# Scatters and gathers alternated by column in the first edge stage of a four-layer graph network, and VectorE's broadcast columns read as per-partition scalars

## The chip, the cores and the metric

The kernel runs on one core of a Trainium2 chip. The metric is the device time of one execution in microseconds (us), the median of several runs. Before the change three runs gave 5754.19, 5760.32 and 5761.99 us.

## The reference, cut to what matters

Four graph layers run one after the other on 3125 nodes of 128 features and 100,000 edges sorted by destination. Each layer gathers a row per edge from a table of the nodes, computes on it, and sums or maximises the rows by destination. Two parts matter here.

```python
# layer 0: both directions of every edge, so one sum is by dst and one by src
mi  = concat([node[src_bi], node[tgt_bi], ef_bi], 1)
h   = relu(layernorm(mi @ w1 + b1)) @ w2 + b2
agg = segment_sum(h, tgt_bi)
# layer 1: a softmax over the edges of one source, summed by destination
seg_max = segment_max(e, src);  p = exp(e - seg_max[src]);  p = p / segment_sum(p, src)[src]
agg = segment_sum(norm_h[src] * p[:, None], dst)
```

The source statistics that layer 1 needs (maximum, sum of exponentials) are collected while layer 0 walks over the edges.

## The kernel before, in words

The edges are padded to 784 columns of 128. A batch is four columns (CB = 4, 512 edges), so a stage over the edges has 196 batches (NBAT); two batches are a group (C2 = 8 columns). Each of the five engines has an order of work written out by hand: one loop over i, in which batch i - k is handled by step k of the pipeline, with semaphores between engines. Nothing is planned at run time.

**First edge stage (`L0_edges`).** GpSimd (POOL) issues indirect DMAs. `pool_gather` (line 1180) fetches, for each of the 128 edges of a column, a row of 256 floats of the table T0 into the ring `Gs` of eight buffers; the first gather of a batch waits until TensorE has read the buffer's previous batch (`T`). `pool_scatter` (line 1161) adds a column of 132 floats per edge into one of three tables `tabs`, chosen by column number modulo three; each scatter waits until the one three columns earlier has landed (`tab`), and the first of a batch waits for its data (`X`, written by ScalarE, lines 1075 and 1076). In round i POOL issues the four scatters of batch i - 9, then `pool_outside` (for this data one no-op that sets `ok`, line 1174), then the four gathers of batch i. Rounds 0 to 8 have no scatters, rounds 196 to 204 no gathers. Rounds 1 to 6 also issue a few small gathers (`pool_sub`, line 1187).

ScalarE's round begins with `act_X`, which waits for all four scatters of the batch three earlier, because the buffer `X2` has three parts. VectorE (DVE) adds the gathered rows to TensorE's products (`dve_t`, line 875), builds a mask of equal sources within a column (`dve_S1`, line 892), scales five of the eight half columns by their rstd (`dve_D`, line 951; ScalarE does the other three), and in every second round builds the one-hot matrices for the source statistics (`dve_A`, lines 956 to 964). In `dve_S1`, `dve_D` and `dve_A` a column of one number per edge is spread over a whole tile by the helper `bf`, as the second input of a `tensor_tensor`; `bc` repeats a row. Line 974 (`dve_OT`) already uses a `tensor_scalar` with a per-partition scalar.

**Second edge stage (`L1_edges`).** Of every seven batches POOL gathers six with line 1525 (`edge_gather`, ring of eight buffers), the seventh comes from TensorE by one-hot matrices. `dve_scale` (line 1733) multiplies the gathered 512 numbers per partition by a broadcast column `pp`; it is followed, in every second round, by lines 1737 and 1741. The third and fourth edge stages use line 1525 too.

Of the kernel before, what the change touches and what calls it, by code (L numbers as in the profile page):

```python
# [6 lines left out]
P = 128  # L7
N = 3125
NBLK = 25
# [5 lines left out]
CB = 4  # L15
C2 = 2 * CB
C4 = 4 * CB
NBAT = NCH // CB
# [3 lines left out]
KT = 3  # L22
# [13 lines left out]
ALU = mybir.AluOpType  # L36
# [115 lines left out]
def bc(v, n=NBLK):  # L152
    return v.unsqueeze(1).to_broadcast([P, n, v.shape[1]])


def bf(v, f=P):
    return v.unsqueeze(2).to_broadcast([P, v.shape[1], f])
# [6 lines left out]
def at_rows(ap):  # L164
    return bass.IndirectOffsetOnAxis(ap=ap, axis=0)
# [17 lines left out]
def build(nc, A, out):  # L183
    with ExitStack() as ctx:
# [10 lines left out]
        arena = Arena(sb("arena", [AW]), AW)  # L195
# [7 lines left out]
        iotaf = sb("iotaf", [P])  # L203
# [478 lines left out]
        def L0_edges():  # L682
# [28 lines left out]
            mg = [arena.get(C2) for _ in range(4)]  # L711
            sg = [arena.get(C2) for _ in range(4)]
            OL = arena.get(C2, P)
            OH = arena.get(C2, NBLK)
            fst = arena.get(C2)
            RH = arena.get(C2, 2, NBLK)
            DM = [arena.get(C2 + 1, NBLK) for _ in range(2)]
            DS = [arena.get(C2 + 1, NBLK) for _ in range(2)]
# [167 lines left out]
            def dve_S1(e, b):  # L886
                g, h0 = b // 2, b % 2 * CB * P
                if b % 2 == 0:
                    e.wait_ge(ld_s.of(g), ld_s.at(g))
                if b >= 6:  # L890
                    e.wait_ge(SS.of(0), SS.at(b - 6))
                e.tensor_tensor(Sm[b % 6], sR[g % 3][:, h0:h0 + CB * P].rearrange("p (c f) -> p c f", f=P),
                                bf(srcF[:, CB * b:CB * b + CB]), ALU.is_equal).then_inc(S1.of(0), 1)

            def dve_dm(e, b):
                g = b // 2
# [50 lines left out]
            def dve_D(e, b):  # L947
                g, o = b // 2, b % 2 * C2
                e.wait_ge(rs.of(0), rs.at(g * (RS + 1) + RS))
                t = Gs[b % NR].rearrange("p c (h f) -> p (c h) f", h=2)[:, 0:C2 - ND, :]  # L950
                e.tensor_tensor(t, t, bf(rst[g % 3][:, o:o + C2 - ND]), ALU.mult).then_inc(D.of(0), 1)

            def dve_A(e, b):
                g = b // 2
                sl = slice(C2 * g, C2 * g + C2)
                e.tensor_tensor(OL, bc(iotaf[:, :], C2), bf(loF[:, sl]), ALU.is_equal)
                e.tensor_tensor(OH, bc(iotaf[:, 0:NBLK], C2), bf(hiF[:, sl], NBLK), ALU.is_equal)
                e.tensor_scalar(fst, cb[g % 4], 0.5, None, ALU.is_lt).then_inc(A1.of(0), 1)
                e.wait_ge(A1.of(0), A1.at(2 * g))
                e.tensor_tensor(OH, OH, bf(fst, NBLK), ALU.mult).then_inc(A1.of(0), 1)  # L960
                e.wait_ge(A1.of(0), A1.at(2 * g + 1))
                e.wait_ge(ex.of(0), ex.at(b))
                e.tensor_tensor(RH[:, :, 0, :], OH, bf(mg[g % 4], NBLK), ALU.mult)
                e.tensor_tensor(RH[:, :, 1, :], OH, bf(sg[g % 4], NBLK), ALU.mult).then_inc(RHd.of(0), 1)

            def dve_S4(e, b):
                e.wait_ge(S3.of(0), S3.at(b))
# [184 lines left out]
                    if 0 <= i - 7 < NBAT and (i - 7) % 2:  # L1152
                        act_DX(e, i - 7)

            def pool_scatter(e, b):
                e.wait_ge(X.of(0), X.at(b))
                for c in range(CB):
                    k = CB * b + c
                    if k >= KT:
                        e.wait_ge(tab.of(k), tab.at(k - KT))  # L1160
                    e.indirect_dma_start(out=tabs[k % KT], out_offset=at_rows(iA[b % 10][:, c:c + 1]),  # L1161
                                         in_=X2[b % 3][:, c, :], in_offset=None, compute_op=ALU.add
                                         ).then_inc(tab.of(k), 16)

            def pool_outside(e, b, some):
                with e.If(some > 0):
# [6 lines left out]
                    e.wait_ge(gx.of(0), gx.at(b))  # L1173
                e.engine_nop().then_inc(ok.of(0), 1)  # L1174

            def pool_gather(e, b):
                if b >= NR:
                    e.wait_ge(T.of(0), T.at(b - NR))
                for c in range(CB):
                    e.indirect_dma_start(out=Gs[b % NR][:, c, :], out_offset=None, in_=T0,  # L1180
                                         in_offset=at_rows(srcI[:, CB * b + c:CB * b + c + 1])
                                         ).then_inc(gs.of(b), 16)

            def pool_sub(e, b0, b1):
                dFc = dF.rearrange("(s i) -> s i", i=P)
# [5 lines left out]
            def pool(e):  # L1191
                meet(e)
                some = e.value_load(flag[0:1, 0:1], min_val=0, max_val=EP)
                for i in range(NBAT + 9):
                    if i == 9:
                        e.wait_ge(st_zero.of(0), st_zero.at(KT - 1))
                    if 0 <= i - 9 < NBAT:
                        pool_scatter(e, i - 9)
                    if 0 <= i - 1 < NBAT:
                        pool_outside(e, i - 1, some)  # L1200
                    if i < NBAT:
                        pool_gather(e, i)
                    if 1 <= i <= 6:
                        pool_sub(e, 4 * (i - 1), 4 * i + (i == 6))
                for k in range(NCH - KT, NCH):
                    e.wait_ge(tab.of(k), tab.at(k))
# [408 lines left out]
        def L1_edges():  # L1615
# [114 lines left out]
            def dve_scale(e, b):  # L1730
                g_ = rows_of(b)
                e.wait_ge(ex.of(0), ex.at(b))
                e.tensor_tensor(g_[:, :, 0:P], g_[:, :, 0:P], bf(pp[b % 4]), ALU.mult).then_inc(D.of(0), 1)

            def dve_cut_r(e, g):
                e.wait_ge(c1.of(0), c1.at(g))
# [768 lines left out]
```

## Time and profile before

| | us |
|---|---|
| median of three runs | 5760.32 |
| the profiled execution's own time | 5759.2 |
| its span, first to last instruction | 5757.4 |
| POOL busy | 4263.1 (74%) |
| TensorE matmuls busy | 4205.9 (73%) |
| VectorE busy | 4170.5 (72%) |
| ScalarE busy | 3607.3 (63%) |

The span holds the preparation of the edge lists, four edge stages and four short node stages. In the profile the first edge stage runs from about 50 to 2692 us (scatters from 151.5 us, gathers until 2622 us), the second from 2799 to about 3687 us, the third from 3754 to about 4780 us and the fourth from 4860 to about 5700 us. A POOL interval in the trace is the time in which GpSimd writes the descriptors of one indirect DMA; the data lands later, and is not part of it. "issue" is idle time that nothing in the profile explains.

### The profile page before, as it was taken

How to read it: one execution, taken by the hardware profiler on the slowest of the kernel's cores; microseconds unless marked ns; L12 is line 12 of the kernel's file. 1: busy time of each engine (PE TensorE's matmuls, PEld its weight loads, DVE VectorE, ACT ScalarE, POOL GpSimd, SP SyncE). 2: the span in 40 equal slices, each digit the busy share in tenths (PEclk: the TensorE clock that was granted, in tenths of full speed). 3: DMA queues.
4: the chain of work that ended last, by engine and by line, in shares of the span. 5: the costliest groups of instructions: out<-in, count | busy, mean ns of one | idle time of the engine just before them, and what ended most of it. 6: DMA issues, size and time to landing. Idle time of an engine off the chain costs nothing.

```text
span 5757.4 us, 83215 instructions
## 1 busy us (share of the span) xinstructions
PE 4205.9 (73%) x23301; PEld 3141.9 (55%) x23378; DVE 4170.5 (72%) x10652; ACT 3607.3 (63%) x12260; POOL 4263.1 (74%) x3819
## 2 busy tenths in 40 slices
PE   3766666676666666665688888658888886999995
PEld 2656666565656565654455555435555554545453
DVE  4877677777777777774788888757777776777776
ACT  3766676767666666763477777447676763555553
POOL 4788888888888888887477777567777763777776
PEclk6877778777777777777799998879999997999997
DMA  8876767676666667675367767456666762555553
GB/s 253 168 170 161 173 159 174 160 169 163 166 167 165 167 162 170 163 171 99 100 192 195 194 197 195 140 169 213 210 211 209 213 198 72 157 156 161 160 158 107
DMA packets 629376, 976.86 MB, mean 170 GB/s; under 512 B 105688, under 2 KB 339026, under 8 KB 628642
## 3 DMA queue, kind: packets, MB, share of 16 engines
q1 hardware_dynamic: 394242, 616.02, 33.9%
q0 software_dynamic: 234656, 355.35, 29.8%
q8 instruction: 192, 3.15, 0.2%
q14 instruction: 286, 2.34, 0.1%
HBM read 668.28 MB, written 306.11 MB: 169 GB/s over the span
## 4 chain that ended last, share of the span: by engine, by line
POOL 60%; issue 21%; PE 6%; DMA 4%; DVE 4%; SPq 1%; POOLq 1%; ACT 1%; DVEq 0%; ACTq 0%
POOL arena L1525 32%; POOL tab L1161 16%; POOL arena L1180 12%; DMA tab<-arena 2%; DMA arena<-T,srcI 1%; POOLq L1174 1%; PE PS L2012 1%; PE PS L1688 1%; POOL arena L1213 1%; PE PS L301 1%; PE PS L1483 0%; SPq L786 0%; PE PS L1990 0%; PE PS L813 0%; PE PS L833 0%
## 5 line engine op out<-in xcount | busy, mean ns | idle before, releaser
L1525 POOL DMA_INDIRECT arena<-T,srcI x2112 | 2034.7, 963 | 787.7 <-issue 636.3
L1161 POOL DMA_INDIRECT tab<-arena x784 | 1290.3, 1646 | 276.9 <-issue 231.1
L1180 POOL DMA_INDIRECT arena<-T,srcI x784 | 804.5, 1026 | 285.6 <-issue 282.2
L1512 DVE TENSOR_TENSOR_SCAN arena<-arena,PS 128x512 f32<-128x512 bf16 x588 | 748.9, 1274 | 183.4 <-PE PS L2326 81.5
L852 PE MATMUL PS<-arena 128*128 128x128 f32 x1568 | 308.7, 358 | 679.7 <-ACT arena L1108 679.7
L1492 ACT ACTIVATE arena<-PS 128x512 f32<-128x512 f32 x588 | 347.4, 591 | 642.8 <-PE PS L1483 642.8
L1592 DVE TENSOR_SCALAR arena<-PS,nodeid 128x512 bf16<-128x512 f32 x908 | 627.9, 739 | 75.4 <-PE PS L1573 75.4
L852 PEld LDWEIGHTS PS<-arena 128*128 128x128 f32 x1568 | 265.8, 256 | 719.0 <-ACT arena L1108 719.0
L933 DVE CUSTOM_DVE_ANT_0 arena<-arena,ltri 128x128 f32<-128x128 f32 x784 | 225.1, 287 | 495.4 <-ACT arena L1084 495.3
L833 PE MATMUL PS<-We,arena 65*128 65x256 f32 x1568 | 511.3, 409 | 87.5 <-DVE arena L875 43.6
L1688 PE MATMUL PS<-arena 128*128 128x396 bf16 x2800 | 544.9, 353 | 7.4 <-DVE arena L1592 7.2
L2308 PE MATMUL PS<-arena 128*128 128x512 bf16 x2323 | 545.2, 382 | 4.3 <-issue 0.2
L1075 ACT ACTIVATE arena<-arena 128x4 f32<-128x4 f32 x196 | 40.7, 208 | 756.5 <-DMA tab<-arena 753.1
L835 PE MATMUL PS<-arena 128*128 128x256 f32 x1568 | 490.8, 395 | 0.0
L1126 ACT ACTIVATE arena<-arena 128x128 bf16<-128x128 f32 x1568 | 459.6, 300 | 40.6 <-DVE arena L875 40.6
L1483 PEld LDWEIGHTS PS<-ident,arena 128*128 128x128 f32 x2352 | 289.4, 145 | 323.2 <-issue 264.8
L1483 PE MATMUL PS<-ident,arena 128*128 128x128 f32 x2352 | 371.8, 282 | 120.2 <-ACT arena L1492 118.7
L1688 PEld LDWEIGHTS PS<-arena 128*128 128x128 bf16 x2800 | 289.3, 104 | 218.4 <-issue 50.0
L1612 ACT ACTIVATE arena<-arena,onesF 128x512 bf16<-128x512 f32 x592 | 402.1, 712 | 6.0
L1607 ACT ACTIVATE arena<-arena,minus 128x512 f32<-128x512 f32 x592 | 400.0, 709 | 0.0
L2032 DVE TENSOR_TENSOR arena<-arena,PS 128x1024 f32<-128x1024 f32 x196 | 238.7, 1218 | 218.8 <-DMA arena<-T,srcI 217.8
L2012 PE MATMUL PS<-arena,wA 128*128 128x512 f32 x784 | 392.9, 625 | 0.0
(302 smaller groups left out, 10279.1 us busy)
## 6 DMA issues: line engine op xcount, KB each, us to landing
H<-arena SPq DMA_DIRECT2D x784, 256.0 KB, 2.5
arena<-keepR SPq DMA_DIRECT2D x294, 256.0 KB, 5.0
arena<-sF SPq DMA_DIRECT2D x98, 512.0 KB, 5.6
arena<-wF SPq DMA_DIRECT2D x98, 512.0 KB, 7.1
arena<-dF SPq DMA_DIRECT2D x98, 512.0 KB, 8.5
arena<-T,srcI POOLq DMA_INDIRECT x2896, 3.5
arena<-in_ea64T SPq DMA_DIRECT2D x98, 256.0 KB
arena<-S SPq DMA_DIRECT2D x98, 256.0 KB
```

The lines of the kernel that those rows point to most:

```text
L833: e.matmul(psC[:, c * 2 * P:(c + 1) * 2 * P], eT[g % 3][0:65, h0 + c * P:h0 + (c + 1) * P], We[0:65, :], start=True, stop=False)
L835: ins = e.matmul(psC[:, c * 2 * P:(c + 1) * 2 * P], OT[b % 2][:, c * P:(c + 1) * P], Tw[g % 4], start=False, stop=True)
L852: ins = e.matmul(bank(6)[:, c * P:(c + 1) * P], Sm[b % 6][:, c, :], R2[b % 2][:, c, :], start=True, stop=True)
L1126: ins = e.activation(ja[:, 2 * c + hh, :], t[:, c, hh * P:(hh + 1) * P], ACT.Square, accum_out=var[g % 3][:, i:i + 1])
L1161: e.indirect_dma_start(out=tabs[k % KT], out_offset=at_rows(iA[b % 10][:, c:c + 1]), in_=X2[b % 3][:, c, :], in_offset=None, compute_op=AL ...
L1180: e.indirect_dma_start(out=Gs[b % NR][:, c, :], out_offset=None, in_=T0, in_offset=at_rows(srcI[:, CB * b + c:CB * b + c + 1])).then_inc(g ...
L1483: ins = e.transpose(psB[b % n][:, (c * nh + h) * P:(c * nh + h + 1) * P], s[b % len(s)][:, h, c * P:(c + 1) * P], ident[:, :])
L1512: ins = e.tensor_tensor_scan(s[b % n][:, h, :], kR[g % 6][:, h0:h0 + CB * P], src[h], s[(b - 1) % n][:, h, CB * P - 1:CB * P] if b else in ...
L1525: e.indirect_dma_start(out=dst[:, c, :], out_offset=None, in_=T_tab, in_offset=at_rows(srcI[:, CB * b + c:CB * b + c + 1])).then_inc(gs.of ...
L1592: e.tensor_scalar(self.OH[j % 2][:, n, :], self.sB[j % len(self.sB)], nodeid[:, n:n + 1], None, ALU.is_equal).then_inc(self.oh.of(0), 1)
L1688: ins = e.matmul(psP[:, c, 0:3 * XW], pk.OH[j % 2][:, n, c * P:(c + 1) * P], part[:, n, :, :].rearrange("p k f -> p (k f)"), start=(n == 0 ...
L2308: ins = e.matmul(bank(4 + j % 2), part[k][:, n, :], pk.OH[j % 2][:, n, :], start=(n == 0 and k == 0), stop=(n == NBLK - 1 and k == 2))
```

## The change

In `L0_edges`, scatters and gathers are issued in turn, column by column, after `pool_outside`, which was between them before. The three VectorE steps replace one wide `tensor_tensor` by one `tensor_scalar` per column (four in `dve_S1`, five in `dve_D`, eight for `OL` in `dve_A`), whose scalar is the column itself. In `dve_A` the matrix `OH` is gone: two small products `first` (eight columns by two) are made instead, and eight `scalar_tensor_tensor` of 50 elements write `RH` directly. In `L1_edges`, `dve_scale` is split in four `tensor_scalar` in the same way.

```diff
@@ dve_S1
-                e.tensor_tensor(Sm[b % 6], sR[g % 3][:, h0:h0 + CB * P].rearrange("p (c f) -> p c f", f=P),
-                                bf(srcF[:, CB * b:CB * b + CB]), ALU.is_equal).then_inc(S1.of(0), 1)
+                for c in range(CB):
+                    k = CB * b + c
+                    ins = e.tensor_scalar(Sm[b % 6][:, c, :], sR[g % 3][:, h0 + c * P:h0 + (c + 1) * P], srcF[:, k:k + 1],
+                                          None, ALU.is_equal)
+                ins.then_inc(S1.of(0), 1)
@@ dve_D
-                t = Gs[b % NR].rearrange("p c (h f) -> p (c h) f", h=2)[:, 0:C2 - ND, :]
-                e.tensor_tensor(t, t, bf(rst[g % 3][:, o:o + C2 - ND]), ALU.mult).then_inc(D.of(0), 1)
+                t = Gs[b % NR].rearrange("p c (h f) -> p (c h) f", h=2)
+                for k in range(C2 - ND):
+                    ins = e.tensor_scalar(t[:, k, :], t[:, k, :], rst[g % 3][:, o + k:o + k + 1], None, ALU.mult)
+                ins.then_inc(D.of(0), 1)
@@ dve_A
-                sl = slice(C2 * g, C2 * g + C2)
-                e.tensor_tensor(OL, bc(iotaf[:, :], C2), bf(loF[:, sl]), ALU.is_equal)
-                e.tensor_tensor(OH, bc(iotaf[:, 0:NBLK], C2), bf(hiF[:, sl], NBLK), ALU.is_equal)
                 e.tensor_scalar(fst, cb[g % 4], 0.5, None, ALU.is_lt).then_inc(A1.of(0), 1)
+                for c in range(C2):
+                    k = C2 * g + c
+                    e.tensor_scalar(OL[:, c, :], iotaf[:, :], loF[:, k:k + 1], None, ALU.is_equal)
                 e.wait_ge(A1.of(0), A1.at(2 * g))
-                e.tensor_tensor(OH, OH, bf(fst, NBLK), ALU.mult).then_inc(A1.of(0), 1)
+                e.wait_ge(ex.of(0), ex.at(b))
+                e.tensor_tensor(first[:, :, 0], fst, mg[g % 4], ALU.mult)
+                e.tensor_tensor(first[:, :, 1], fst, sg[g % 4], ALU.mult).then_inc(A1.of(0), 1)
                 e.wait_ge(A1.of(0), A1.at(2 * g + 1))
-                e.wait_ge(ex.of(0), ex.at(b))
-                e.tensor_tensor(RH[:, :, 0, :], OH, bf(mg[g % 4], NBLK), ALU.mult)
-                e.tensor_tensor(RH[:, :, 1, :], OH, bf(sg[g % 4], NBLK), ALU.mult).then_inc(RHd.of(0), 1)
+                for c in range(C2):
+                    k = C2 * g + c
+                    ins = e.scalar_tensor_tensor(out=RH[:, c, :, :], in0=bc(iotaf[:, 0:NBLK], 2), scalar=hiF[:, k:k + 1],
+                                                 in1=bf(first[:, c, :], NBLK), op0=ALU.is_equal, op1=ALU.mult)
+                ins.then_inc(RHd.of(0), 1)
@@ pool, L0_edges (pool_scatter and pool_gather now take one column c; their waits on X and T stand at c == 0)
-                    if 0 <= i - 9 < NBAT:
-                        pool_scatter(e, i - 9)
                     if 0 <= i - 1 < NBAT:
                         pool_outside(e, i - 1, some)
-                    if i < NBAT:
-                        pool_gather(e, i)
+                    for c in range(CB):
+                        if 0 <= i - 9 < NBAT:
+                            pool_scatter(e, i - 9, c)
+                        if i < NBAT:
+                            pool_gather(e, i, c)
@@ dve_scale, L1_edges
-                e.tensor_tensor(g_[:, :, 0:P], g_[:, :, 0:P], bf(pp[b % 4]), ALU.mult).then_inc(D.of(0), 1)
+                for c in range(CB):
+                    ins = e.tensor_scalar(g_[:, c, 0:P], g_[:, c, 0:P], pp[b % 4][:, c:c + 1], None, ALU.mult)
+                ins.then_inc(D.of(0), 1)
```

## Rows read from the trace of the kernel before

**Rows 1.** Windows of both stages: length, busy us of PE, PEld, DVE, ACT, POOL
```profile
151.00:2622.00 2471.00, 1658.18 (x9080) 1494.76 (x9079) 1793.47 (x7004) 1700.41 (x7665) 2001.17 (x1496) 0.78 0.69 165
2799.00:3673.00 874.00, 743.67 (x4381) 473.94 (x4381) 713.85 (x1189) 629.49 (x1278) 669.20 (x672) 0.91 0.68 190
```
**Rows 2.** The chain that ended last, whole span, by engine
```profile
POOL 60%; issue 21%; PE 6%; DMA 4%; DVE 4%; SPq 1%; POOLq 1%; ACT 1%; DVEq 0%; ACTq 0%
```
**Rows 3.** Who waited for whom, 300 to 2600 us: total, times, longest
```profile
ACT arena L1075 <- DMA tab<-arena: 691.7, 88, 9.7
...
POOL tab L1161 <- DMA tab<-arena: 7.5, 17, 1.6
```
**Rows 4.** Timeline of POOL, mid-stage: start, length, instruction, idle before
```profile
1427.70 1.61 POOL L1161 DMA_INDIRECT tab<-arena  x1 [0.30 <-issue]
1429.62 1.57 POOL L1161 DMA_INDIRECT tab<-arena  x1 [0.30 <-issue]
1431.49 1.56 POOL L1161 DMA_INDIRECT tab<-arena  x1 [0.30 <-issue]
```
**Rows 5.** Timeline of POOL: the first gathers after the stage's last scatters
```profile
2700.62 1.02 POOL L1213 DMA_INDIRECT arena<-H,endI  x1 [8.90 <-POOLq L276]
2701.95 0.98 POOL L1213 DMA_INDIRECT arena<-H,endI  x1 [0.30 <-issue]
2703.23 0.94 POOL L1213 DMA_INDIRECT arena<-H,endI  x1 [0.30 <-issue]
```
**Rows 6.** Timeline at 362 to 367 us, two rows of DVE, two of POOL
```profile
362.30 0.82 DVE L951 TENSOR_TENSOR arena<-arena 128x640 f32<-128x640 f32 x1
...
362.67 1.87 POOL L1161 DMA_INDIRECT tab<-arena  x1 [0.30 <-issue]
...
366.52 1.22 DVE L875 TENSOR_TENSOR arena<-arena,PS 128x1024 f32<-128x1024 f32 x1 [1.69 <-POOLq L1174]
...
366.71 1.02 POOL L1180 DMA_INDIRECT arena<-T,srcI  x1 [0.31 <-issue]
```
**Rows 7.** Timeline at 485 us, a per-partition scalar instruction and a gather
```profile
485.56 0.48 DVE L974 TENSOR_SCALAR arena<-arena,wcol 128x512 f32<-128x512 f32 x1
485.80 1.14 POOL L1180 DMA_INDIRECT arena<-T,srcI  x1 [0.30 <-issue]
```
**Rows 8.** Groups by form, 300 to 2600 us: busy us, mean ns, idle before
```profile
L1161 POOL DMA_INDIRECT tab<-arena x699 | 1152.2, 1648 | 215.5 <-issue 207.3 <-DMA tab<-arena 7.5 <-ACT arena L1076 0.6
L1180 POOL DMA_INDIRECT arena<-T,srcI x700 | 720.7, 1030 | 213.3 <-issue 210.3 <-PE PS L813 2.4 <-DMA tab<-arena 0.6
...
L951 DVE TENSOR_TENSOR arena<-arena 128x640 f32<-128x640 f32 x176 | 143.6, 816 | 0.0
...
L892 DVE TENSOR_TENSOR arena<-arena,srcF 128x512 f32<-128x512 f32 x175 | 119.9, 685 | 4.6 <-PE PS L852 4.5
...
L956 DVE TENSOR_TENSOR arena<-iotaf,loF 128x1024 f32<-128x1024 f32 x88 | 107.1, 1217 | 0.0
...
L960 DVE TENSOR_TENSOR arena<-arena 128x200 f32<-128x200 f32 x88 | 32.3, 367 | 3.0
```
**Rows 9.** Timeline of DVE outside the stages: two lone forms and a run of 25
```profile
2710.50 0.29 DVE L1410 TENSOR_SCALAR arena<-onesF,cols 128x128 f32<-128x128 f32 x1
2710.70 0.28 DVE L281 TENSOR_REDUCE small<-wA 128x1 f32<-128x128 f32 x1
...
2729.15 6.65 DVE L1291 SCALAR_TENSOR_TENSOR arena<-vec,small,arena 128x128 f32<-128x128 f32 x25
```
**Rows 10.** Line 1161, whole span: us and times idle until a landing
```profile
  DMA tab<-arena: 20.7, 23
```
**Rows 11.** Timeline in the second stage: three DVE instructions and one gather
```profile
2875.75 0.68 DVE L1733 TENSOR_TENSOR arena<-arena 128x512 f32<-128x512 f32 x1
2875.77 2.15 POOL L1525 DMA_INDIRECT arena<-T,srcI  x1 [0.30 <-issue]
...
2876.69 0.41 DVE L1741 TENSOR_TENSOR arena<-arena 128x256 bf16<-128x256 f32 x1
```

More of the change, by code:

```diff
@@ L713, in L0_edges @@
             OL = arena.get(C2, P)
-            OH = arena.get(C2, NBLK)
-            fst = arena.get(C2)
+            fst, first = arena.get(C2), arena.get(C2, 2)
             RH = arena.get(C2, 2, NBLK)
@@ L1153, in act, with pool_scatter @@
                         act_DX(e, i - 7)
[L1155 to L1163, printed above, removed]
+            def pool_scatter(e, b, c):
+                k = CB * b + c
+                if c == 0:
+                    e.wait_ge(X.of(0), X.at(b))
+                if k >= KT:
+                    e.wait_ge(tab.of(k), tab.at(k - KT))
+                e.indirect_dma_start(out=tabs[k % KT], out_offset=at_rows(iA[b % 10][:, c:c + 1]),
+                                     in_=X2[b % 3][:, c, :], in_offset=None, compute_op=ALU.add
+                                     ).then_inc(tab.of(k), 16)
             def pool_outside(e, b, some):
@@ L1174, in pool_outside, with pool_gather @@
                 e.engine_nop().then_inc(ok.of(0), 1)
-            def pool_gather(e, b):
-                if b >= NR:
+            def pool_gather(e, b, c):
+                if c == 0 and b >= NR:
                     e.wait_ge(T.of(0), T.at(b - NR))
[L1179 to L1182, printed above, removed]
+                e.indirect_dma_start(out=Gs[b % NR][:, c, :], out_offset=None, in_=T0,
+                                     in_offset=at_rows(srcI[:, CB * b + c:CB * b + c + 1])).then_inc(gs.of(b), 16)
             def pool_sub(e, b0, b1):
```

## The prediction

> **What bounds the kernel now.** I read the chain of waits first: POOL holds 60% of it and "issue" another 21% [rows 2]. The windows show what "issue" is. Between 151 and 2622 us POOL is busy 2001 us in 1496 indirect DMAs; every one has 0.30 us before it, and 2001 + 1496 x 0.305 = 2457 of 2471 us. In the second stage 669 + 672 x 0.305 = 874 of 874 [rows 1]. So in both stages that the change touches POOL writes descriptors without a pause, and the stage lasts as long as its POOL instructions do. What the other engines do there costs only what it does to POOL. They are far ahead: ScalarE stands idle 692 us until scatters land, while POOL waited for a landing 17 times, 7.5 us in all [rows 3].
>
> So the question is what makes a POOL instruction long. Two things do.
>
> First, **a change of kind**. The first scatter behind gathers takes 1.61 us, the second 1.57, later ones about 1.55 [rows 4]. The first gather behind scatters takes 1.02 us, the second 0.98, the next 0.94, even when 8.9 us of idle time lie between [rows 5]. A change to scatters costs 0.065 (and 0.015 on the second), a change to gathers 0.075 (and 0.035 on the second). A round has one of each: 0.19 us.
>
> Second, **some DVE instructions keep POOL from starting**. The scatter that began 0.37 us into line 951 took 1.87 us, 0.32 more than its 1.55; line 951 had 0.45 us to go. The gather that began inside line 875, which reads PSUM, took its 1.02 [rows 6]. So it is not a busy DVE that costs, but a tensor_tensor with both inputs in SBUF, and the loss is what is left of it less 0.12 us (0.45 - 0.12 = 0.33). I went through the starts of the first stage in the timeline: 95 lie in line 951, and for all the loss is this difference within hundredths.
>
> **Port waits removed.** Rounds with both kinds are 187 long (scatters begin at 151.5 us, gathers end at 2622), 2471/187 = 13.2 us each, and POOL starts 8 times in one, 0.606 per us. Starts being taken as random in time, an instruction of length d costs on average (d - 0.12)^2/2 x 0.606 per occurrence. With the means of [rows 8]: line 951 0.243, line 892 0.159, line 956 every second round 0.60/2, and four of 0.36 us every second round (line 960 stands for 957, 963, 964) 4 x 0.029/2. Sum 0.759 x 0.606 = 0.46 us a round, x 187 = **86 us**. Check: POOL's means of 1.648 and 1.030 make 4 x 2.678 = 10.71 us a round; without port waits it would be 1.61 + 1.57 + 2 x 1.55 + 1.02 + 0.98 + 2 x 0.945 = 10.17. The difference, 0.54, also holds what other DVE lines cost.
>
> **Port waits put in their place.** A per-partition scalar on a 128x128 tile takes 0.29 us and the next instruction starts 0.20 us after it [rows 9]. Does it keep POOL out as well? Line 974 has this form at 512 columns: the gather that began 0.24 us into its 0.48 took 1.14 instead of 1.02, 0.12 more, and 0.24 - 0.12 = 0.12 [rows 7]. So the form is not free, only short: what is left of 0.29 us, less 0.12. Averaged over starts 0.205 us apart that is 0.168^2/2 = 0.014 per instruction. A round gets 4 + 5 + 8/2 = 13 of them, and 8/2 scalar_tensor_tensor of 50 elements; at 128 elements that form goes at 6.65/25 = 0.266 us each [rows 9], the slope between lines 892 and 956 (1217 - 685 ns for 512 elements) takes 0.08 off for the 78 fewer, so 0.185 apart and, with the 0.08 of overlap, 0.265 long: 0.145^2/2 = 0.0105 each. Sum 13 x 0.014 + 4 x 0.0105 = 0.225 x 0.606 = 0.14 a round, **26 us**. This holds if POOL gets in between two of a train. It is bounded from above by trains that hold POOL out until their end: 0.90, 1.11 and, every second round, 1.72 and 1.53 us, (0.304 + 0.490 + 1.137) x 0.606 x 187 = 219 us; and from below by 0. I take 26, because line 956 directly behind 951 never prolonged a wait. But [rows 11] shows that it can: the gather at 2875.77 took 2.15 us, 1.21 over 0.94, and that is the end of line 1741 (2877.10) less 0.12, two instructions after the one it met. About ten of 54 starts in line 1733 with line 1737 behind it went so.
>
> The Trainium skill (SBUF — State Buffer, the practical consequences listed with its port table) says that a tensor_scalar in a 2-port mode shuts GpSimd out of the shared pair for the whole instruction, while a tensor_tensor with two SBUF inputs only contends with a GpSimd instruction that reads SBUF. Read strictly this speaks against the change, since it puts the stronger lock in place of the weaker. The trace agrees that line 974 locks, and gives it the same price per us left [rows 7]; by the rule's "whole instruction" alone the sum stays as above.
>
> **Alternation.** A round gets four changes of each kind instead of one: 3 x (0.065 + 0.075) = 0.42, less the second-instruction extras (0.05) = 0.37 us, x 187 = **69 us** added. Bounds: nothing of it recurs and even the 0.19 of now goes (-36 us); or every instruction pays both extras, 4 x 0.19 - 0.19 = 0.57, 107 us. I take the first extra and not the second: 8.9 idle us did not take the cost away [rows 5], so it hangs on which kind ran last and not on time, and there will be no second instruction of a kind in a row. That one instruction of the other kind costs as much as four is my assumption; no row shows it. What alternation gives: scatter k waits for k - 3, which is now 3 x 3.2 = 9.7 us earlier instead of 5.6. A landing was late by a mean of 0.9 us in 23 cases, 20.7 us in all [rows 10]; 4 us more room takes nearly all of them, I count **18 gone**. The last scatter of a batch is 3.6 us later in the round, and with it ScalarE's round; its 692 idle us, 7.9 per two rounds, move with it. POOL waited 0.6 us for X and 2.4 us for T in 2300 us [rows 8], and a shift of 3.6 us is less than the 7.9, so I expect neither to become late. The no-op ahead of the scatters sets ok some 8 us earlier; DVE waited for it at line 875 (one such wait, 1.69 us, stands in [rows 6]), but POOL not for DVE: nothing.
>
> **DVE's own time.** dve_S1 4 x 0.205 for 0.60 (start to start), dve_D 5 x 0.205 for 0.73, dve_A 3.4 for 2.6 every second round: +0.22 +0.30 +0.4 = 0.9 us on 1793/187 = 9.6, 10.5 of 13 us. Hidden under POOL; uncovered it would cost 0.9 x 187 = 170 us. The bound from the other side is that the smaller forms overlap better, nothing gained.
>
> **Second stage.** POOL starts once per 1.30 us. Line 1733 (0.684) costs 0.159/1.30 x 196 = 24 us [rows 11]; four scalars 4 x 0.014/1.30 x 196 = 8.5: **15.5 us gained**. With whole trains (0.90) 46, so 22 lost. DVE gets 0.22 x 196 = 43 us on 714 of 874, hidden.
>
> **Sum.** -86 + 26 + 69 - 18 - 15.5 = -24.5 us on the profiled execution's own 5759.2 (span 5757.4 and 1.8 around it): 5734.7. The median of the runs is 1.1 us above it, so about **5735**, 0.4% faster.
>
> **Rivals.** (1) *Changing kind is cheap when it is frequent*: the cost seen may come from four of one kind in a row. Then 69 falls away and perhaps 36 more: 5630 to 5666, say 5650. For: the second instruction of a kind is nearly back to normal after a single one, so little has to be brought back and it may survive one instruction of the other kind. Against: the size is the same for any gap in time [rows 5]. (2) *Trains shut POOL out*, the slower case: 219 for 26 and 46 for 8.5 add 231: 5965. It decides from the share of starts in a train that wait it out; 24.5/231 = 11% makes the gain nothing. For: [rows 11], against: 951 with 956. A half-way share of 40% gives 5827. (3) *Every change costs both extras*: +38, 5773. For: the second instruction's extra is there in [rows 4, 5]. (4) *DVE sets the round*: TensorE, ScalarE and DVE hand a batch round in a loop over two rounds, and its 7.9 us of slack shrink by about 2. It decides from a slack below 0; against it are the 692 us; 1% slower, 5800.
>
> The Trainium skill (VectorE: DVE Perf Modes, the errata section) adds that a fixed latency is paid per SBUF instruction and that tiles under 512 elements are to be avoided. By that rule alone DVE's 0.9 us a round is the whole change and a loss; the trace has that price too, but covers it.
>
> **How the numbers follow.** My forecast 46%, rival 1 18%, 2 17%, 3 14%, 4 5%. Within 0.2%, or 11.5 us, a measurement of this kernel can't tell a change. Faster: three quarters of my forecast (35) + 18 = 52%, a little less for rival 1's mild form; same: 9 of my forecast + 8 of rival 3 = 17%; slower: the rest, 31%. The likeliest case's own range is 5705 to 5765. For 8 in 10 the range takes in the near half of rivals 1 and 2: 5650 to 5840.
>
> **What would show it.** Right: POOL still with 0.30 us before every instruction from 151 us on; a round of 13.15 us (the 9 us that the first stage gains are 0.05 a round); scatters at 1.61, gathers at 1.02 at best, means near 1.64 and 1.05; hardly a wait for a landing; the second stage at 858 us; DVE at 10.5 us a round. Wrong: gathers at 0.94 in an alternating row (rival 1); scatters or gathers 0.5 to 1.5 us longer that end with a train (2); gathers at 1.06 (3); POOL idle until ScalarE or TensorE (4).

## The result, and the profile after

The changed kernel takes 5702.5 us (median of four runs, 5700.0 to 5705.4) where the kernel before, run beside it, takes 5758.7: ratio 0.990 (95% interval 0.9886 to 0.992). The forecast was 5735. The direction was right and the time lies in the range of 5650 to 5840 (2.5 us below the 5705 to 5765 of the likeliest case), but the gain is 56 us and not 24.5.

First the windows of the kernel after, as [rows 1]: length, then busy us of PE, PEld, DVE, ACT and POOL. The ends are chosen anew, from the first scatter to the last gather of the first stage, and for the second stage.

```profile
155.00:2583.00 2428.00, 1648.85 (x9065) 1493.49 (x9064) 1969.85 (x9554) 1709.20 (x7652) 1943.40 (x1497) 0.77 0.72 168
2757.00:3617.00 860.00, 735.41 (x4385) 470.14 (x4386) 749.39 (x1768) 627.15 (x1278) 654.16 (x672) 0.93 0.70 194
```

The first stage went from 2471 to 2428 us, the second from 874 to 859. POOL still fills both: 1943 + 1497 x 0.305 = 2400 of 2428 in the first, 654 + 672 x 0.305 = 859 of 860 in the second. DVE rose to 1970/187 = 10.5 us a round, as forecast, and nobody waits for it.

Next the groups of POOL by form, 300 to 2600 us, which answer to the first two of [rows 8]:

```profile
L1169 POOL DMA_INDIRECT tab<-arena x717 | 1135.9, 1584 | 235.2 <-issue 205.7 <-DMA tab<-arena 29.5
L1187 POOL DMA_INDIRECT arena<-T,srcI x707 | 715.9, 1013 | 215.4 <-issue 202.6 <-DMA tab<-arena 6.7 <-PE PS L812 6.1
```

A scatter costs 1.584 us instead of 1.648, a gather 1.013 instead of 1.030; but idle time put down to landings rose from 8 to 36 us. (Each such idle holds the 0.30 us that stand before every instruction; above these the whole stage had 29 us of waiting in 37 places, before the change 14 us in 8.)

The timeline of POOL in the middle of the stage, beside [rows 4]:

```profile
1426.87 0.99 POOL L1187 DMA_INDIRECT arena<-T,srcI  x1 [0.30 <-issue]
1428.16 1.58 POOL L1169 DMA_INDIRECT tab<-arena  x1 [0.30 <-issue]
1430.05 1.04 POOL L1187 DMA_INDIRECT arena<-T,srcI  x1 [0.30 <-issue]
1431.39 1.58 POOL L1169 DMA_INDIRECT tab<-arena  x1 [0.30 <-issue]
```

Undisturbed, an alternating scatter takes 1.577 and a gather 0.988. The forecast had 1.61 and 1.02.

And what DVE does to POOL now, the timeline at 446 us and two rounds later; this pattern comes up again below:

```profile
446.38 1.58 POOL L1169 DMA_INDIRECT tab<-arena  x1 [0.30 <-issue]
...
446.89 1.25 DVE L954 TENSOR_SCALAR arena<-arena 128x128 f32<-128x128 f32 x5
448.06 0.22 DVE L976 TENSOR_SCALAR arena<-arena,pcol 128x4 int32<-128x4 f32 x1
448.19 0.48 DVE L982 TENSOR_SCALAR arena<-arena,wcol 128x512 f32<-128x512 f32 x1
448.26 1.27 POOL L1187 DMA_INDIRECT arena<-T,srcI  x1 [0.30 <-issue]
...
472.13 1.58 POOL L1169 DMA_INDIRECT tab<-arena  x1 [0.30 <-issue]
...
472.65 1.24 DVE L954 TENSOR_SCALAR arena<-arena 128x128 f32<-128x128 f32 x5
473.81 0.22 DVE L976 TENSOR_SCALAR arena<-arena,pcol 128x4 int32<-128x4 f32 x1
473.94 0.47 DVE L982 TENSOR_SCALAR arena<-arena,wcol 128x512 f32<-128x512 f32 x1
474.02 1.26 POOL L1187 DMA_INDIRECT arena<-T,srcI  x1 [0.31 <-issue]
```

### The profile page after: what moved, and what is told of

It is laid out like the page before. It is cut to its first block, busy times and chain, and to the rows that moved or that the text cites. A ratio compares the mean times of both kernels' runs of the same rounds, so it can differ in the third digit from the quotient of the medians.

```text
span 5702.3 us, 86525 instructions
## 1 busy us (share of the span) xinstructions
PE 4191.3 (74%) x23378; PEld 3139.7 (55%) x23378; DVE 4391.8 (77%) x13886; ACT 3617.3 (63%) x12260; POOL 4185.1 (73%) x3819
## 4 chain that ended last, share of the span: by engine, by line
POOL 48%; issue 20%; DMA 12%; PE 10%; DVE 6%; ACT 2%; SPq 1%; POOLq 0%; DVEq 0%; ACTq 0%
POOL arena L1532 28%; POOL tab L1169 11%; POOL arena L1187 9%; DMA tab<-arena 9%; PE PS L1695 3%; DMA arena<-T,srcI 2%; PE PS L2021 1%; PE PS L1490 1%; PE PS L812 1%; PE PS L301 1%; PE PS L832 1%; PE PS L1999 1%; POOL arena L1220 1%; PE PS L834 1%; SPq L785 0%
## 5 line engine op out<-in xcount | busy, mean ns | idle before, releaser
L1169 POOL DMA_INDIRECT tab<-arena x784 | 1241.2, 1583 | 295.8 <-issue 223.1
L812 PE MATMUL PS<-ident,arena 128*128 128x128 f32 x1568 | 293.6, 349 | 249.3 <-DVE arena L992 249.3
L1490 PE MATMUL PS<-ident,arena 128*128 128x128 f32 x2352 | 370.7, 282 | 108.1 <-ACT arena L1499 106.9
```

Source lines behind the costliest of these rows:

```text
L1490: ins = e.transpose(psB[b % n][:, (c * nh + h) * P:(c * nh + h + 1) * P], s[b % len(s)][:, h, c * P:(c + 1) * P], ident[:, :])
```

## Experiments

All were made with one account of the first stage. POOL's instructions are sorted by place, which is their own kind and the kinds of the three before them. The length that a fifth of a place's instructions stay under (the 20% quantile) is its floor. What an instruction takes above its floor is called a port wait and goes to the DVE instruction running when it starts; what lies between two instructions above 0.305 us is a wait. The table is worked out from the timelines: stage from first scatter to last gather; floors of eight instructions; port waits from 300 to 2600 us; waits over the stage. The times are medians of runs on several chips, beside which the kernel before took 5758 to 5766 us. The ratios in the text allow for that and the times in the table don't, so a few us between two rows of it mean nothing.

| kernel | time, us | stage, us | floors a round | port waits | waits |
|---|---|---|---|---|---|
| before | 5758.7 | 2471 | 10.16 | 96 | 14 |
| after | 5702.5 | 2427 | 10.26 | 23 | 29 |
| alternation alone | 5782.7 | 2494 | 10.28 | 85 | 22 |
| after, block order | 5705.6 | 2424 | 10.17 | 33 | 32 |
| after, in pairs | 5746.7 | 2480 | 10.38 | 22 | 61 |
| after, dve_A wide | 5774.6 | 2490 | 10.26 | 84 | 26 |
| before, dve_A short | 5734.8 | 2451 | 10.17 | 67 | 21 |
| after, four tables | 5683.2 | 2403 | 10.26 | 23 | 5 |
| block order, four tables | 5677.2 | 2396 | 10.15 | 33 | 6 |
| four tables, s s s g g g s g | 5669.4 | 2393 | 10.20 | 25 | 3 |
| block, four tables, dve_OT cut | 5664.9 | 2389 | 10.16 | 27 | 6 |

It closes: after, 187 x 10.26 + 1496 x 0.305 + 23 x 187/178 + 29 = 2428 of 2427; before 2471 of 2471; the other kernels within 5 us. That shows that nothing is left out. It doesn't show that the split is right, since whatever is no floor and no gap is a port wait by definition.

**Alternation alone** (the order of the change in the kernel before, its DVE instructions untouched).

```diff
-    if 0 <= i - 9 < NBAT: pool_scatter(e, i - 9)
     if 0 <= i - 1 < NBAT: pool_outside(e, i - 1, some)
-    if i < NBAT: pool_gather(e, i)
+    for c in range(CB):
+        if 0 <= i - 9 < NBAT: pool_scatter(e, i - 9, c)
+        if i < NBAT: pool_gather(e, i, c)
```

> The kernel before with only the order of POOL's queue changed in the first stage: the no-op first, then scatter and gather in turn by column; VectorE keeps its wide tensor_tensor instructions. Theory A (the gain is VectorE's short instructions; alternation costs): in the changed kernel an undisturbed scatter takes 1.577 us and an undisturbed gather 0.988, against 1.61, 1.57, 1.55, 1.55 and 1.02, 0.98, 0.94, 0.94 before, 0.12 us a round more, 22 us; waits for landings add about 20 us; the long port waits stay near 80 us. So 5758 + 22 + 20 = about 5800 us, slower. Rival B (alternation made the gain, because it frees scatters from waiting and spreads POOL's starts): 5758 - 40 = about 5718 us, and the wide instructions cost little when scatters and gathers alternate.

5782.7 us, ratio 1.003 (1.0019 to 1.0042): a loss of about 19 us, between the two expectations and nearer the first (5800). By the table kinds add 187 x 0.117 = 22, port waits fall by 11 (other instructions are met), waits rise by 8.

**Block order** in the changed kernel (the reverse of that diff).

> The changed kernel with POOL's queue in the first stage back in its old order (four scatters, the no-op, four gathers); VectorE keeps the short instructions in both stages. Theory A: the port waits stay as small as in the changed kernel (0.13 us a round against 0.54 before), the change of kind costs 0.19 us a round instead of 0.31, and three of four scatters have the four gathers between themselves and the one they wait for. So 5702 - 22 for the kinds and - 20 for landings: about 5660 us, faster than the changed kernel. Rival B: alternation made the gain; without it landings are waited for at the first pair of every block as POOL gets faster, and the time goes back to 5740 or more (only the second stage's 15 us are kept).

5705.6 us, ratio 0.989 (0.9875 to 0.9905): neither. With short instructions the order is worth nothing: its kinds cost 0.09 us a round (17 us) less, its port waits 10 us more, spread over several DVE lines (dve_OT's and dve_S2's take 4 of them). The whole gain of the change is in the DVE instructions: alone the order loses 19 us, and on top of the short instructions it changes nothing that the runs can tell.

**Second stage alone** (dve_scale as in the change, all else as before).

> The kernel before with only dve_scale of the second edge stage split into four per-partition scalar instructions. Theory A: the gathers that start inside the instruction wait at most 0.17 us instead of 0.56, so the mean of the second stage's gathers falls by 0.023 us, 672 of them, 15 us: 5743 us. Rival C (the short instructions follow each other so closely that POOL does not get in between them): up to 22 us slower, 5780 us.

5752.2 us, ratio 0.998 (0.9971 to 0.9989). The groups of line 1525 in that stage, before and with this edit:

```profile
L1525 POOL DMA_INDIRECT arena<-T,srcI x669 | 666.4, 996 | 203.9 <-issue 200.5 <-PE PS L1699 3.4
```
```profile
L1525 POOL DMA_INDIRECT arena<-T,srcI x672 | 653.8, 973 | 272.8 <-issue 202.8 <-SPq L276 68.1 <-PE PS L1699 1.8
```

A gather costs 0.973 instead of 0.996 and the stage 858.4 instead of 873.6 us: 15 us, as expected; the whole run is 11 us shorter than the kernel before beside it. (The 68 us are the pause ahead of the stage, inside this window only.) The first stage of that execution was 6 us longer without any edit in it.

**Trains and a wide instruction by themselves.** Into the kernel before, whose third and fourth stage hold no such work, eight more `tensor_scalar` of 128x128 a round (third) and one more `tensor_tensor` of 128x1024 (fourth).

```diff
@@ third stage
+    for c in range(C2):
+        ins = e.tensor_scalar(spare[:, c, :], iotaf[:, :], srcF[:, c:c + 1], None, ALU.is_equal)
@@ fourth stage
+    e.tensor_tensor(spare, bc(iotaf[:, :], C2), bf(srcF[:, 0:C2]), ALU.is_equal)
```

> A measurement of the port wait alone, in the kernel before: in the third stage VectorE also executes eight per-partition scalar instructions of 128x128 one after the other in every round, in the fourth stage one tensor_tensor with two SBUF inputs of 128x1024 in every round (results unused). In the kernel before no gather of these two stages was prolonged (0.942 to 0.950 us). Theory A: a gather that starts inside the train waits at most 0.17 us, whatever its place in the train; one that starts inside the wide instruction (1.22 us) waits for what is left less 0.12, up to 1.1 us. Mean excess per start hit: 0.07 us and 0.55 us. Rival C: a gather that meets the train waits until the train's end, up to 1.6 us.

It ran once, in 5977 us, and only the lengths of the gathers in these two stages are read from it. Two gathers that met a train, and one that met the wide instruction, in the timeline:

```profile
3844.47 1.25 DVE L2068 TENSOR_SCALAR arena<-iotaf,srcF 128x128 f32<-128x128 f32 x6
3844.54 1.03 POOL L1525 DMA_INDIRECT arena<-T,srcI  x1 [0.30 <-issue]
...
3854.64 1.15 DVE L2068 TENSOR_SCALAR arena<-iotaf,srcF 128x128 f32<-128x128 f32 x5
3854.74 0.99 POOL L1525 DMA_INDIRECT arena<-T,srcI  x1 [0.30 <-issue]
```
```profile
5440.42 1.22 DVE L2356 TENSOR_TENSOR arena<-iotaf,srcF 128x1024 f32<-128x1024 f32 x1
5440.57 1.88 POOL L1525 DMA_INDIRECT arena<-T,srcI  x1 [0.30 <-issue]
```

Of 302 gathers begun inside a train the mean is 0.981 us against 0.945, the longest excess 0.22: 0.04 a hit, and no train of 1.7 us was waited out. Of 166 begun inside the wide instruction the mean is 1.416, an excess of 0.47, the longest above 1.0. That settles, for trains of this form, the rival in which trains shut POOL out. The Trainium skill (SBUF — State Buffer, the terms at its head) has the shared port pair held "for the full instruction"; the trace agrees, for one instruction at a time: between two `tensor_scalar` of a train POOL gets in. (Where a two-input `tensor_tensor` comes next it does not always; see dve_A wide again.) Its other condition, that a tensor_tensor with two SBUF inputs contends only with a GpSimd instruction that reads SBUF, is no protection here: the wide one is a tensor_tensor, and it cost 0.47 us a hit. Whether POOL reads SBUF while it writes these descriptors (the gather's row numbers, `srcI`, stand there) no run shows.

**In pairs** (s s g g s s g g, s a scatter, g a gather).

```diff
-    for c in range(CB): scatter(c); gather(c)
+    for c0 in range(0, CB, 2):
+        scatter(c0); scatter(c0 + 1); gather(c0); gather(c0 + 1)
```

> The changed kernel with POOL's queue as two scatters, two gathers, two scatters, two gathers. It shows how the price of a change of kind depends on what ran before. If the price is per change and grows with the number of the other kind in a row (undisturbed scatter 0.032 us more after one gather, 0.065 after four; gather 0.045 after one, 0.075 after four), the first of a pair lies between the two and the second is a little above the steady 1.545 and 0.945: four first and four second instructions, about 0.25 us a round over steady, between 0.19 (block) and 0.31 (alternating). The time then follows the waits for landings: 5700 to 5708 us by either theory. If instead every change costs 0.065 and 0.075 as in my prediction, the alternating kernel was helped by something else, and here a round is 0.30 over steady.

5746.7 us, ratio 0.997 (0.9954 to 0.9978), some 40 us worse than expected. The groups of POOL, 300 to 2600 us:

```profile
L1169 POOL DMA_INDIRECT tab<-arena x696 | 1119.0, 1608 | 262.2 <-issue 186.5 <-DMA tab<-arena 70.2 <-ACT arena L1084 5.5
L1187 POOL DMA_INDIRECT arena<-T,srcI x695 | 707.0, 1017 | 211.9 <-issue 211.3 <-PE PS L812 0.6
```

and a piece of its timeline:

```profile
1402.96 1.02 POOL L1187 DMA_INDIRECT arena<-T,srcI  x1 [0.30 <-issue]
1404.29 0.98 POOL L1187 DMA_INDIRECT arena<-T,srcI  x1 [0.30 <-issue]
1405.58 1.61 POOL L1169 DMA_INDIRECT tab<-arena  x1 [0.31 <-issue]
1408.54 1.57 POOL L1169 DMA_INDIRECT tab<-arena  x1 [1.34 <-DMA tab<-arena]
1410.41 1.02 POOL L1187 DMA_INDIRECT arena<-T,srcI  x1 [0.30 <-issue]
1411.74 0.98 POOL L1187 DMA_INDIRECT arena<-T,srcI  x1 [0.30 <-issue]
```

Two things. Every first instruction of a pair pays the full price, 1.61 and 1.02, every second a part, 1.57 and 0.98. Over the steady 4 x (1.545 + 0.945) = 9.96 that makes 0.42 a round, where the two theories had 0.25 and 0.30; it is 0.12 a round above alternation, 22 us. And there are 32 us more of waits for landings: for every second scatter the one three earlier began 8.4 us before, while in alternation it is always 9.6. In the trace after, a scatter lands a median of 3.6 us after its start, but one in ten takes over 8.8 and one in fifty over 9.8, so 9.6 is nearly enough and 8.4 is not. (This profiled execution, 5758.0, is 11 us above the median, so the split is shown better than the size.)

**A fourth table** (KT = 4), in the changed kernel and in block order.

```diff
-KT = 3
+KT = 4
```

> The changed kernel with KT = 4: four scatter tables instead of three, so scatter k waits for k - 4; the node stage loads and sums one more table. Theory A: the waits for landings in the first stage, 29 us between the first scatter and the last gather of the changed kernel, go almost entirely, since the landing then has 12.9 us instead of 9.7; the fourth table costs 3 to 6 us in the node stage and one more clearing. So 5702 - 25 + 5 = about 5682 us. Rival D (the waits are caused by queues of the DMA engines, and fewer waits only lead to later landings): 5702 to 5710 us.

> The changed kernel with POOL's queue in the old block order and KT = 4. Theory A: as with the old order and three tables (5705.6 us), less its 32 us of waits for landings, plus 5 for the fourth table: about 5680 us, equal to the alternating kernel with four tables or a few us better, because the change of kind costs 0.09 us a round less. Rival D: 5705 to 5712 us.

5683.2 us (ratio 0.986, 0.9842 to 0.987) and 5677.2 (0.985, 0.9834 to 0.9859), both as expected. The waits go from 29 and 32 us to 5 and 6. So landings, which the forecast had as a gain of alternation, are worth some 20 to 28 us in either order once the rounds are short.

**dve_A wide again** in the changed kernel.

> The changed kernel with dve_A alone put back to its wide instructions (one of 1024 and four of 200 elements); dve_S1 and dve_D stay short. Theory A: these instructions held POOL 0.36/2 x 0.61 = 0.22 us a round in the prediction's working, their short forms 0.04 by the probe; so 0.18 x 187 = 34 us of the gain go: about 5735 us. Rival C (DVE's added time, 0.45 us a round for dve_A, matters): part of that comes back, 5710 us or less.

5774.6 us, ratio 1.002 (1.0009 to 1.0027): one of the five edits undone costs 72 us by the medians and 66 by the ratios, where 34 were expected, and more than the whole change brings. The timeline at two places:

```profile
1441.59 1.58 POOL L1166 DMA_INDIRECT tab<-arena  x1 [0.30 <-issue]
...
1443.27 1.21 DVE L961 TENSOR_TENSOR arena<-iotaf,loF 128x1024 f32<-128x1024 f32 x1
1443.47 2.17 POOL L1184 DMA_INDIRECT arena<-T,srcI  x1 [0.30 <-issue]
...
1444.40 0.36 DVE L962 TENSOR_TENSOR arena<-iotaf,hiF 128x200 f32<-128x200 f32 x1
...
1468.26 1.58 POOL L1166 DMA_INDIRECT tab<-arena  x1 [0.30 <-issue]
...
1469.94 1.21 DVE L961 TENSOR_TENSOR arena<-iotaf,loF 128x1024 f32<-128x1024 f32 x1
1470.14 2.17 POOL L1184 DMA_INDIRECT arena<-T,srcI  x1 [0.30 <-issue]
...
1471.08 0.35 DVE L962 TENSOR_TENSOR arena<-iotaf,hiF 128x200 f32<-128x200 f32 x1
```

The wide instruction begins 0.20 us before the gather, again and again (53 of 87 times): 84 POOL starts lie in it, with 0.81 us each, 68 us. In the kernel before the same instruction (line 956) was met 40 times at 0.54, 21 us.

The lengths shown also break the rule of the prediction. With 1.01 us left of the wide instruction the gather should have lost 1.01 - 0.12 = 0.89; it lost 1.18. That is the end of the next instruction, line 962 (1444.76), less the same 0.12. Of the 84 gathers 40 were held through line 962 as well, about 0.29 us each, 12 of the 68 us. In the kernel before the same two instructions stand one behind the other, and none of the 40 starts there was held past the first. [rows 11] shows the other case on record, and the second stage of the trace after still has 17 such gathers, three of them begun in the last `tensor_scalar` of a train and held through the two `tensor_tensor` behind it. In all of these the next instruction is a `tensor_tensor` with two SBUF inputs; a start held by short ones alone lost 0.22 us at most. What decides whether POOL gets in between is open.

**dve_A short alone** in the kernel before.

> The kernel before with dve_A alone in short form (eight per-partition comparisons in place of the 128x1024 one, eight scalar_tensor_tensor). In the trace before, dve_A's wide instructions made 40 starts wait at 0.54 us, 21.4 us, and its 128x200 ones 5.4 us more, 29 us over the whole stage. Theory A (the waits of each instruction stand by themselves): 5759 - 29 + 3 = 5733. Theory B (the rhythm decides which instruction the starts fall on; with dve_A short, dve_D's and dve_S1's wide ones are met more or less often): the result departs from 5733 by more than 8 us, and the trace shows other hit counts on the 128x640 and the 128x512 instruction than 88 and 115.

5734.8 us, ratio 0.995 (0.994 to 0.9967), as the first theory has it. But the hits moved too: starts that lost over 0.02 us in line 951's instruction (L950 here) were 69 instead of 88, in line 892's (L891 here) 63 instead of 99. The total fell by 29 us as computed; the shares of the single instructions did not stand still. This execution's own time, 5751, is 16 us above the median, so its counts are an indication only.

**dve_A wide, but ahead of dve_D.**

```diff
-    dve_D(e, i - 5)
     if (i - 5) % 2: dve_A(e, i - 5)
+    dve_D(e, i - 5)
```

> The changed kernel with dve_A wide again, as in the run that took 5774.6 us, but dve_A stands ahead of dve_D in VectorE's order instead of behind it. There the 128x1024 instruction stood in the way of 84 of the 86 gathers after a batch's last scatter, 0.81 us each, 68 us between 300 and 2600 us, because it began 0.20 us before that gather again and again. Theory A (what counts is where the instruction stands against POOL's starts, and VectorE's round keeps step with POOL's): it now begins about 1.2 us earlier, inside a scatter of 1.58 us, and ends before the gather starts, which then meets a 128x200 instruction at 0.24 at most; 45 to 65 us less, 5710 to 5730. Theory B (the form costs this much wherever it stands): 5775.

This run fell on a chip on which the kernel before takes 6357 us, so only the ratio and the first stage can be compared; POOL's undisturbed instructions there are 1.577 and 0.992. Ratio 0.997 (0.9959 to 0.9985) where dve_A behind dve_D had 1.002, 26 us less where 45 to 65 were expected; the stage 2443 us where that had 2490. POOL met the wide instruction 30 times instead of 84, 24 us instead of 68. In 57 of 89 cases no POOL start falls into it, as here, where it is over when the gather starts:

```profile
1484.26 1.22 DVE L961 TENSOR_TENSOR arena<-iotaf,loF 128x1024 f32<-128x1024 f32 x1
...
1485.63 0.99 POOL L1184 DMA_INDIRECT arena<-T,srcI  x1 [0.30 <-issue]
```

The same instruction, as many times, at less than half the price. What changed is how often it was met and by what: here all 30 starts in it are scatters, at 0.79 us each and none held past it, there all 84 were gathers. So where it stands against POOL's starts sets what it costs. That its place in VectorE's order was what moved it is likely, but not shown: the chip changed together with the order, other engines may keep another pace on it, and dve_A behind dve_D did not run there. The details were not as expected: it did not always start inside a scatter, and where it came 0.36 us before one, that took 2.31.

**Threes and ones** (s s s g g g s g, four tables).

> Four tables, every short instruction, and the order s s s g g g s g in each round (s scatter, g gather). Theory A (the price of a mixed order depends on the two instructions before: about 0.03 to 0.04 where the one before is of the other kind, and about as much again where the second one before is): the scatter after a single gather that follows a scatter 1.577, the second 1.56 to 1.57, the third 1.55, the scatter after three gathers 1.61; gathers 1.02 after three scatters, 0.98, 0.946, and 0.988 after the single scatter; floors of 10.23 a round, time 5681, between block order (5677) and alternation (5683). Theory B (each change of kind costs the same, 0.065 for a scatter and 0.075 for a gather): 1.61 and 1.02 after every change, 10.31 a round, 5690 or more.

5669.4 us, ratio 0.984 (0.9829 to 0.9859), 12 us better than expected. Some 7 of them are the chip: the kernel before took 5758.5 beside this run, and 5765.7 beside the runs that the expectation was built on. The durations are those of the first theory:

```profile
1402.91 1.61 POOL L1169 DMA_INDIRECT tab<-arena  x1 [0.30 <-issue]
1404.83 0.98 POOL L1187 DMA_INDIRECT arena<-T,srcI  x1 [0.30 <-issue]
1406.11 1.58 POOL L1169 DMA_INDIRECT tab<-arena  x1 [0.30 <-issue]
1408.00 1.57 POOL L1169 DMA_INDIRECT tab<-arena  x1 [0.30 <-issue]
1409.87 1.55 POOL L1169 DMA_INDIRECT tab<-arena  x1 [0.31 <-issue]
1411.73 1.02 POOL L1187 DMA_INDIRECT arena<-T,srcI  x1 [0.30 <-issue]
```

1.61 only where both instructions before are gathers, 1.58 where one is. The floors are 10.20 a round, where the theories had 10.23 and 10.31. Against block order with four tables the ratios (0.984 and 0.985, intervals overlapping) show no gain: the stage is 2 us shorter, with fewer port waits (25 for 33) against the dearer kinds.

**dve_OT cut in four** (block order, four tables).

```diff
-    e.tensor_scalar(OT[b % 2], dR[...][:, h0:h0 + CB * P], wcol[:, g:g + 1], None, ALU.is_equal)
+    for c in range(CB):
+        ins = e.tensor_scalar(OT[b % 2][:, c * P:(c + 1) * P], dR[...][:, h0 + c * P:h0 + (c + 1) * P], wcol[:, g:g + 1], None, ALU.is_equal)
```

> Block order, four tables and every short instruction as in the best version so far (5677.2 us), and dve_OT's instruction of 128x512 cut into four of 128x128. In that version's trace this instruction stood in the way of 48 GpSimd starts between 300 and 2600 us at 0.23 us each, 11.1 us, about 12 over the stage. Theory A (a start waits for what is left of the VectorE instruction running then, so cut pieces cost 0.02 to 0.04 a hit): 9 to 11 us less, 5667 to 5669. Theory B (cutting adds 4 x 0.30 - 0.49 = 0.7 us to VectorE's round of some 11 us in 12.8, and that side sets the round or shifts costlier instructions into the starts): no gain or a loss, 5677 to 5700.

5664.9 us, ratio 0.984 (0.9822 to 0.9849). This is the fastest version that ran, 38 us below the changed kernel. Against the same without the cut the medians say 12 us and the ratios 6, with intervals that overlap; in the traces, one of each, dve_OT's port waits went from 11 to 4 us and the stage is 7 us shorter. A gain of some 6 us is thus what the traces support and the runs by themselves don't show.

## Why the prediction was right or wrong

The account of the profiled executions, whose spans are 5757.4 and 5702.3: first stage -44, its start 3.5 later, the scatters after it -2, second stage -15, the stretch between +1. These add up to -56, the spans differ by 55. Against the terms of the forecast: port waits removed 3 us less than said, short instructions 19 cheaper, the changes of kind 49 cheaper, landings 33 dearer. That the time is only 32 us from the forecast, with one term 49 off, is owed in part to luck: the landings took back 33.

**What bounds the kernel: right.** In every row of the table POOL's instructions and the 0.305 us between them fill the stage but for 3 to 61 us of waits.

**Port waits removed, -86: right.** Lines 951, 892, 956, 964 and 960 had 79 us between 300 and 2600 us, 83 over the stage. As a sum over instructions the random-start estimate held; for one alone it doesn't (the 128x1024 instruction: 21 us in the kernel before, 68 in the changed kernel, 24 ahead of dve_D). That line 956 behind 951 never prolonged a wait is true of that trace, and no rule: 40 gathers were held through two instructions with dve_A wide.

**Put in their place, +26: too high.** The four new lines (893, 954, 962, 970) cost 7 us. The starts that fell on them were about as many as assumed: 385 of 1424, where 3.4 of 13 us would give 373. But each lost 0.02 us on average where the estimate had 0.07. It had every instruction cost most at its beginning; in the trace after, the 81 starts in the first 0.07 us of an instruction of lines 893, 954 and 962 lost nothing on average. Why is open (in the probe such starts lost 0.05). The bound of 219 is refuted by the probe.

**Alternation, +69: this step failed.** The prediction took the first extra in full at each change and named the assumption: "one instruction of the other kind costs as much as four is my assumption; no row shows it". The runs show the extra to be made of two parts. Where the instruction before is of the other kind a scatter pays 0.03 and a gather 0.04. Where only the second one before is, a gather pays 0.036 and a scatter 0.01 to 0.03; where both are, 0.065 and 0.075. Four gathers and then a scatter: both parts, 1.61; one gather between scatters: one part, 1.577; second scatter after gathers: the other, 1.56 to 1.57. Alternation pays 4 x (0.032 + 0.042) = 0.30 a round, block order 0.19: 0.11 and not 0.37, x 187 = 20 us. Pairs pay 0.42, 0.03 more than the parts add up to. The account was fitted on three orders and then held on a fourth, for each length to 0.011 us. So what came was about half way from the likeliest case to the first rival, and the 49 us between 69 and 20 are the largest of the errors.

**Landings, -18: wrong in sign, +15.** That scatter k - 3 is "now 9.7 us earlier instead of 5.6" is true of one column in four. For the other three the gathers lie between, and the median in the trace before is 11.0 to 11.2 us; alternation takes them down to 9.6. And shorter rounds shrink every such distance: block order with short instructions waits 32 us where the kernel before waited 14. A gain in one term of the sum was partly given back in another that the prediction had held fixed.

**Second stage, -15.5: right**, 15. **DVE's own time: right**, 10.5 us a round, hidden. dve_OT cut in four adds another 0.4 us a round and is hidden as well.

Of the signs, the round was to be 13.15 and is 2427/187 = 12.98; scatters 1.61 and gathers 1.02 at best were wrong; the second stage at 858 and DVE at 10.5 came true.

## What to carry to other kernels

Where GpSimd writes descriptors without a pause, cut VectorE's SBUF work into short instructions: the cost of a hit is mostly what is left of one instruction, and here 17 short ones a round cost a twelfth of the wide ones they replaced. Look in the timeline for starts that are held through two instructions, above all where a two-input `tensor_tensor` follows directly. If two engines keep step, a random-start estimate gives the sum and not the single instruction: read where each one starts against the other engine, and try another place for it. After a stage has been made shorter, add up the distances between reuse of a buffer again; the fourth table brought 20 to 28 us that were not there before.

## What the runs showed of the hardware that was not expected

**The lock works the other way too.** In the trace after, 209 of the 895 instructions of line 954 between 300 and 2600 us took at least 0.05 us more than their median of 0.28, up to 0.60, 44 us more together. Of those held inside a scatter 98 ended 1.11 us after its start and 63, each the next of its train, 1.18 us after it; of those at a gather 14 ended 1.03 us after its start. The rows at 446 and 472 us show what comes of it: the train begins 0.51 us into the scatter and takes 1.25 us for five, and dve_OT's instruction then begins 0.07 us before the next gather, both times. In the run with dve_A wide the same train is followed by the 128x1024 instruction, 0.20 us before the gather. So short instructions are let go by POOL at a fixed point of its own, and what stands behind them in VectorE's order comes at a fixed distance from POOL's next start. That this hold is what keeps the two in step is an argument from these offsets, and no run took the hold away. What the wide instruction costs by where it meets POOL was seen in four traces (40 hits at 0.54 us, 60 at 0.42 with alternation alone, 84 at 0.81, 30 at 0.79).

**A start can be held through more than one instruction.** The rule "what is left, less 0.12 us" fits the 166 hits of the probe to about 0.01 us, and fails for 40 of 84 gathers with dve_A wide and for 10 of 88 in line 1733 of the kernel before, which waited for the end of a second or third `tensor_tensor`. No run isolates the condition.

**A longer memory of kinds than one instruction**, as above, with nothing in the rows that says what is remembered. It reaches past two: a gather behind one scatter takes 0.988 in alternation and 0.977 where three gathers stood before that scatter. The same durations stood on the chip on which the whole kernel took 6357 us, so they do not hang on what makes that chip slow, which these runs leave open.
